# A graph kernel's prologue: four buffers of attribute slices, two of them in A, and the bias of A's tiles added on GpSimd

## The chip, the cores and the metric

The kernel runs on one NeuronCore of a Trainium2 chip. Its metric is the device time of one execution in microseconds (us). Five engines work beside each other, each with its own list of instructions: TensorE (PE, with PEld for its weight loads), VectorE (DVE), ScalarE (ACT), GpSimd (POOL) and SyncE (SP, which here only issues DMAs). They are ordered by semaphores alone.

## The reference

Layer norm and ReLU, then two relational graph layers, then an attention layer over the same edges:

```
edge_type = argmax(edge_attr[:, 16:26])          # one of 10, for 400000 edges
seg  = dst * 10 + edge_type                      # dst is sorted, 12500 nodes
mean = segment_sum(x[src], seg) / max(count(seg), 1)
h    = relu(einsum('nrd,rdo->no', mean, w_rel1) + x @ root1 + b1)
x    = x + (einsum('nrd,rdo->no', mean', w_rel2) + h @ root2 + b2)
x    = x + attention over the same edges          # softmax per destination
```

The kernel first multiplies each node's row by all ten relation weights (a table, ytab) and by the root weight, and then gathers and sums table rows over the edges. An edge's weight is one over the number of edges of its destination and type.

## The kernel before

`prologue()` prepares everything for the first gather pass. Three strands of work run in it at once.

*VectorE, the slices.* The edges lie on 125 partitions, 3200 to each, in 50 slices of 64. A slice holds 64 edges x 42 attributes per partition (1.34 MB in all). SP loads slice t into `ea[t % 2]` by two DMAs (L246) once VectorE has read slice t - 2 (semaphore `s_rel`). VectorE finds the largest of ten attributes (L328), marks it (L329), and turns the mark into a type number (L331 to L333). From slice 5 on, four counts of the edges at a partition's two ends follow (`end_counts`, L321). Between slices stands side work: after slice 1 the destinations (L335 to L349, which wait for dst and for the neighbours' destinations), after slice 3 the step tables (L351 to L380), after slice 6 the sources, and after the slices named in `SHOWN` the statistics of seven tiles of x (L304, L307), with their inverse two slices later.

*VectorE, the rounds.* When all slices are through, the counts are summed (L396), carries between the partitions are made, keys are turned by TensorE and copied by ScalarE (L553, L485), and then ten rounds follow, one for each type: a comparison (L417), a scan forward (L419), a scan backward (L420) and a predicated copy (L422), each over 3200 columns. The rounds 0 to 6 end with the statistics of the next seven tiles, which wait for x. Last come five reciprocals (L430), whose results TensorE turns and ScalarE copies.

*The tile stream.* 98 tiles of 128 nodes, in batches of seven. ScalarE normalizes seven tiles (L458), TensorE turns them (L532) and multiplies each by the ten relation weights and the root weight (L542 to L544), and adds the bias by a product of a row of ones and the bias row (L545). ScalarE copies the ten relation parts to one of two buffers `yb` (L474, L476) and the root part with the bias to A, columns 128 i to 128 i + 127 (L478). GpSimd waits for that and issues the store of `yb` to ytab (L285). ScalarE's copy of tile i waits for the store of tile i - 2 (`s_out`). TensorE's product of tile i waits for ScalarE's last copy of tile i - 2 (`s_y1`). The load of x for batch b + 2 is issued by ScalarE after the fourth tile of batch b. After tile 34 (the end of batch 4) TensorE waits for the end of the slices, for the carries and the keys, before it goes on with tile 35.

Within an engine the order is that of the code. SP's list is one queue of loads: slices, dst, the last destination of each group of 640 edges (625 single elements, L250), the neighbours' destinations (L252, L253), src, and at last the step tables.

`Chain` (called `link`) gives each VectorE instruction a semaphore and waits for it before the next. The gather passes after the prologue start when all engines are through it.

Of the kernel before, what the change touches and what calls it, by code (L numbers as in the profile page):

```python
# [21 lines left out]
ALU = mybir.AluOpType  # L22
# [4 lines left out]
P = 128  # L27
N = 12500
D = 128
# [8 lines left out]
G = 5  # L38
# [6 lines left out]
SHOWN = (7, 15, 23, 31, 39, 46)  # L45
# [38 lines left out]
assert all(BLOCK * (NBLK - 2) + OUT_AT[b] >= GROUPS + OB * b + OB - 1 for b in range(OUTS))  # L84
assert AHEAD == UNROLL and NT % 2 == 0 and STEPS + UNROLL <= SCOLS * P
# [3 lines left out]
def build(nc, x, src, dst, attr, w_rel1, root1, b1, w_rel2, root2, b2, w_l, w_r, att, bias, out,  # L89
# [58 lines left out]
    with outer:  # L148
# [20 lines left out]
        def prologue():  # L169

            with ExitStack() as st:
                ea_all = sbuf(st, "ea", [CH, 2 * EB * ATTR])
                ea = [ea_all[:, k * EB * ATTR:(k + 1) * EB * ATTR] for k in range(2)]
                top = sbuf(st, "top", [CH, EB])
# [30 lines left out]
                brow = sbuf(st, "t1_b", [1, D])  # L205
# [15 lines left out]
                s_ea = [sem(f"ea_in{k}") for k in range(2)]  # L221
                s_dst, s_src, s_nb = sem("dst_in"), sem("src_in"), sem("neighbours_in")
                s_last, s_rel, s_iota = sem("last_in"), sem("ea_used"), sem("iotas")
                s_const, s_raw = sem("prep_const"), sem("raw_free")
# [4 lines left out]
                s_eps, s_w = sem("t1_eps_set"), sem("t1_w_in")  # L229
# [7 lines left out]
                with nc.Block() as block:  # L237

                    @block.sync
                    def _(sp):  # L240
                        av = attr.rearrange("(p t e) a -> p t (e a)", t=CE // EB, e=EB)
                        for t in range(CE // EB):
                            if t >= 2:
                                sp.wait_ge(s_rel, t - 1)
                            for p0, p1 in EA_PARTS:
                                sp.dma_start(ea[t % 2][p0:p1, :], av[p0:p1, t, :]).then_inc(s_ea[t % 2], 16)  # L246
                            if t == 0:
                                sp.dma_start(raw[:, :], dst.rearrange("(p e) -> p e", p=CH)).then_inc(s_dst, 16)
                                with nc.allow_non_contiguous_dma(reason="one destination of each group and chunk"):
                                    sp.dma_start(last_i, dst.rearrange("(a g e) -> a g e", a=1, e=GE)[:, :, GE - 1]).then_inc(s_last, 16)  # L250
                                    sp.wait_ge(s_const, 1)
# [23 lines left out]
                    @block.gpsimd  # L275
                    def _(pool):
                        nc.gpsimd.iota(cols[:, :], [[1, P]], base=0, channel_multiplier=0, allow_small_or_imprecise_dtypes=True).then_inc(s_iota, 1)
                        nc.gpsimd.iota(rowid[:, :], [[0, 1]], base=0, channel_multiplier=1, allow_small_or_imprecise_dtypes=True).then_inc(s_iota, 1)
                        nc.gpsimd.iota(falling[:, :], [[-1, NREL]], base=NREL, channel_multiplier=0, allow_small_or_imprecise_dtypes=True).then_inc(s_iota, 1)
                        nc.gpsimd.iota(gnum, [[1, GROUPS]], base=0, channel_multiplier=0, allow_small_or_imprecise_dtypes=True).then_inc(s_iota, 1)  # L280
                        nc.gpsimd.iota(snum[:, :], [[P, SCOLS]], base=0, channel_multiplier=1, allow_small_or_imprecise_dtypes=True).then_inc(s_iota, 1)
                        nc.gpsimd.memset(rel_all[:, TILES:TILES + SLOTS * G], 0.0).then_inc(s_iota, 1)
                        for i in range(NT):
                            pool.wait_ge(s_y1, i + 1)
                            pool.dma_start(ytab[i * P:(i + 1) * P, :], yb[i % 2]).then_inc(s_out[i % 2], 16)  # L285

                    @block.vector
                    def _(dve):
                        link = Chain(dve, "prep_chain")
                        v = nc.vector  # L290
                        v.memset(eps[:, :], EPS).then_inc(s_eps, 1)
# [32 lines left out]
                        for t in range(CE // EB):  # L324
                            dve.wait_ge(s_ea[t % 2], 16 * len(EA_PARTS) * (t // 2 + 1))
                            a = ea[t % 2][:, :].rearrange("p (e a) -> p e a", a=ATTR)[:, :, EMB:EMB + NREL]
# [7 lines left out]
                            if t == 1:  # L334
                                dve.wait_ge(s_dst, 16)  # L335
                                link(v.tensor_copy(dstc, raw[:, :]))
                                v.engine_nop().then_inc(s_raw, 1)
# [12 lines left out]
                            if t == 3:  # L350
# [30 lines left out]
                            if t == 6:  # L381
# [49 lines left out]

                    @block.scalar
                    def _(act):
# [35 lines left out]
                        def out_rows(i):  # L469
# [7 lines left out]
                            act.wait_ge(s_y0, i + 1)  # L477
                            a.activation(A[:, i * D:(i + 1) * D], py[k][:, NREL * D:ALL], ACT.Copy).then_inc(s_y1, 1)  # L478
# [12 lines left out]
                        act.dma_start(brow[:, :], b1.rearrange("(a d) -> a d", a=1)).then_inc(s_w, 16)  # L491
# [3 lines left out]
                        act.wait_ge(s_eps, 1)  # L495
# [26 lines left out]
                    def _(pe):  # L522
# [12 lines left out]
                        def product(i):  # L535
# [8 lines left out]
                            t.matmul(py[k][:, 1024:ALL], lhs, wt[:, 1024:ALL], start=True, stop=False)  # L544
                            t.matmul(py[k][:, NREL * D:ALL], ones[0:1, :], brow[0:1, :], start=False, stop=True).then_inc(s_m1, 1)  # L545
# [1158 lines left out]
```

## Time and profile before

| | us |
|---|---|
| median of 3 runs | 12709.82 |
| lowest and highest | 12708.29 and 12718.36 |
| the profiled execution | 12666.73 |
| its span | 12664.9 |

The prologue is the first 665 us of the span. Busy over the whole span are TensorE 7165.4 us, VectorE 5372.7, ScalarE 4183.5 and GpSimd 9039.3; nearly all of GpSimd's is the issue of gathers after the prologue. A row of the timeline gives the start in us from the span's start, the duration, the engine, the line, the operation and the tiles it writes and reads; what stands in brackets is the idle time before it and who ended it. A row of waits gives the total in us, how many times, and the longest.

### The profile page before, as it was taken

The page shows a single profiled execution, that of the slowest core. Times are in us where ns is not written, and L with a number is a line of the kernel's source. Part 1 is how long each engine was busy: PE and PEld are TensorE (multiplying, and loading weights), DVE is VectorE, ACT ScalarE, POOL GpSimd, SP SyncE. Part 2 cuts the span into 40 slices and gives each one's busy share as a digit, 9 for nine tenths or more (in the row PEclk, how much of TensorE's full clock was granted, in tenths as well). Part 3 has the DMA queues.
Part 4 walks back from the last instruction along what each step waited for, and adds up shares of the span by engine and source line. Part 5 has one row for each costly group of instructions (what it writes and reads, how often), then busy time and mean ns, then how long its engine had stood idle before and what let it go on. Part 6 is the DMA issues. An engine that isn't in the chain of part 4 may idle for free. (4 is left out here: it accounts for less than half of the span.)

```text
span 12664.9 us, 190403 instructions
## 1 busy us (share of the span) xinstructions
PE 7165.4 (57%) x34895; PEld 5988.6 (47%) x34896; DVE 5372.7 (42%) x11674; ACT 4183.5 (33%) x12473; POOL 9039.3 (71%) x9581
## 2 busy tenths in 40 slices
PE   3734444444444864444444444556777777777777
PEld 1333333333333543333333333445666666666666
DVE  7832222222222641111111111453766766666667
ACT  2522222222222222222222222224444444444442
POOL 0167777777777767777777777767777777777776
PEclk8855555555555975555555555667989999989898
DMA  8611111111112531111111111236888888888887
GB/s 246 207 52 52 53 52 53 52 53 52 53 52 64 187 130 52 53 52 53 52 53 52 53 52 53 75 86 179 236 233 233 237 235 235 235 234 237 233 236 212
DMA packets 922698, 1589.79 MB, mean 126 GB/s; under 512 B 303128, under 2 KB 487318, under 8 KB 915334
## 3 DMA queue, kind: packets, MB, share of 16 engines
q0 software_dynamic: 314112, 685.63, 20.1%
q1 hardware_dynamic: 384568, 595.99, 15.1%
q10 hardware_dynamic: 223412, 301.41, 8.0%
q8 instruction: 219, 3.59, 0.1%
q14 instruction: 387, 3.17, 0.1%
HBM read 1213.18 MB, written 367.39 MB: 125 GB/s over the span
## 5 line engine op out<-in xcount | busy, mean ns | idle before, releaser
L714 POOL DMA_INDIRECT p_g<-ytab,p_i x6250 | 5903.3, 945 | 1971.2 <-issue 1631.1
L1165 POOL DMA_INDIRECT a_g<-xlw,a_i x3125 | 2992.3, 958 | 996.4 <-issue 887.3
L678 PE MATMUL p_pg<-p_v,p_oh 128*128 x6120 | 1343.7, 398 | 1550.4 <-ACT p_v L761 1548.7
L761 ACT ACTIVATE p_v<-p_g,wgt_all 128x128 f32<-128x128 f32 x6250 | 1960.4, 389 | 543.2 <-issue 523.2
L678 PEld LDWEIGHTS p_pg<-p_v,p_oh 128*128 128x128 f32 x6120 | 1203.8, 296 | 1711.3 <-issue 1701.5
L755 ACT ACTIVATE p_i<-rel_all 128x5 int32 (+1 forms) x1250 | 260.1, 208 | 5053.6 <-DMA p_g<-ytab,p_i 5053.6
L678 PE MATMUL p_pt<-p_v,p_oh 128*128 x4200 | 979.8, 417 | 1269.3 <-ACT p_v L761 1269.3
L678 PEld LDWEIGHTS p_pt<-p_v,p_oh 128*128 128x128 f32 x4200 | 877.7, 313 | 1368.3 <-issue 1368.3
L1628 PE MATMUL a_px<-a_g,ident 128*128 x1450 | 736.6, 593 | 849.4 <-SPq L1216 741.2
L616 DVE TENSOR_TENSOR p_oh<-p_cols,local 128x640 f32<-128x640 f32 x1460 | 1195.4, 819 | 24.9
L1264 ACT ACTIVATE a_away<-a_dst,a_minus 128x640 f32 x727 | 602.2, 828 | 1386.7 <-issue 843.5
L635 DVE TENSOR_TENSOR A<-p_pg,A 128x128 f32 x612 | 177.6, 290 | 1988.3 <-PE p_pg L678 1986.6
L1617 PE MATMUL a_pg<-a_v,a_into 128*128 128x132 f32 x7000 | 968.6, 288 | 87.9 <-issue 43.0
L1617 PEld LDWEIGHTS a_pg<-a_v,a_into 128*128 128x128 f32 x7000 | 897.7, 201 | 100.3 <-issue 63.5
L678 PE MATMUL y_py<-p_v,p_oh 128*128 x2080 | 490.0, 420 | 649.5 <-ACT p_v L761 649.5
L635 DVE TENSOR_TENSOR A<-p_pt,A 128x128 f32 x420 | 122.4, 291 | 1669.8 <-PE p_pt L678 1669.5
L678 PEld LDWEIGHTS y_py<-p_v,p_oh 128*128 128x128 f32 x2080 | 438.1, 316 | 699.9 <-issue 699.3
L1634 PEld LDWEIGHTS a_px<-a_xr,a_onto 128*128 128x128 f32 x4350 | 710.4, 220 | 68.4
L1634 PE MATMUL a_px<-a_xr,a_onto 128*128 128x132 f32 x4350 | 707.1, 306 | 0.0
L1628 PEld LDWEIGHTS a_px<-a_g,ident 128*128 128x128 f32 x1450 | 240.0, 207 | 937.6 <-issue 936.7
L1551 DVE TENSOR_TENSOR a_relu<-a_relu,a_pcon 128x640 f32<-128x640 f32 x725 | 587.2, 810 | 175.3 <-ACT a_relu L1314 172.3
L1313 ACT ACTIVATE a_relu<-a_px 128x384 f32<-128x384 f32 x725 | 350.6, 484 | 900.3 <-PE a_py L1634 880.6
(254 smaller groups left out, 9807.6 us busy)
## 6 DMA issues: line engine op xcount, KB each, us to landing
a_xj<-xjw ACTq DMA_DIRECT2D x725, 330.0 KB
xjw<-a_g SPq DMA_DIRECT2D x625, 330.0 KB
a_dst<-in_dst_dram SPq DMA_DIRECT2D x625, 320.0 KB
p_g<-ytab,p_i POOLq DMA_INDIRECT x6250
ytab<-steps POOLq DMA_DIRECT2D x98, 640.0 KB, 3.5
ytab<-src_i SPq DMA_DIRECT2D x98, 640.0 KB
ea<-in_edge_attr_dram SPq DMA_DIRECT2D x50, 1176.0 KB
a_g<-xlw,a_i POOLq DMA_INDIRECT x3125
```

What stands on the lines that cost most here:

```text
L616: v.tensor_tensor(onehot[k][:, :].rearrange("p (t n) -> p t n", t=G), colsp[:, 0:P].rearrange("p (a n) -> p a n", a=1).to_broadcast([P, G, ...
L635: v.tensor_tensor(A[:, ds(to[k], width)], pg[b][:, 0:width], A[:, ds(to[k], width)], ALU.add).then_inc(s_acc, 1)
L678: last = t.matmul(pg[b][:, 0:width], onehot[(at + k) % LOOK][:, q * P:(q + 1) * P], V[:, ds(to + q * width, width)], start=(q == 0), stop= ...
L714: pool.indirect_dma_start(gbuf[k][:, q * D:(q + 1) * D], None, rows, bass.IndirectOffsetOnAxis(ap=stage[k][:, q:q + 1], axis=0)).then_inc( ...
L761: last = a.activation(V[:, c:c + D], gbuf[k][:, q * D:(q + 1) * D], ACT.Copy, scale=wgt[:, ds(G * g + q, 1)])
L1165: pool.indirect_dma_start(gbuf[k][:, q * W:(q + 1) * W], None, xlw, bass.IndirectOffsetOnAxis(ap=stage[k][:, q:q + 1], axis=0)).then_inc(s ...
L1264: a.activation(away[:, :], dall[:, ds(at, GE)], ACT.Abs, bias=minus[:, ds(s, 1)]).then_inc(s_away, 1)
L1313: a.activation(lk[:, 0:HEADT, :], x3[:, :, 0:D], ACT.Relu)
L1551: v.tensor_tensor(lk, lk, attp.rearrange("p (a d) -> p a d", a=1).to_broadcast([P, G, D]), ALU.mult).then_inc(s_wt, 1)
L1617: last = t.matmul(sums(j, b), into[b][:, q * P:(q + 1) * P], V[b][:, q * W:(q + 1) * W], start=(q == 0), stop=(q == G - 1))
L1628: t.matmul(px[b], ident[:, :], gath[:, ds(ring, HEADT * W)], start=True, stop=False)
L1634: last = t.matmul(to, onto[b][:, q * P:(q + 1) * P], xr[k % RING][:, :], start=False, stop=q in (HEADT - 1, G - 1))
```

## The change

Four things change, all in the prologue.

1. Slices go round in four buffers. Two are the old ones, two lie in A's columns of tiles 56 to 97. ScalarE waits for the end of the slices before it writes tile 56.
2. SP issues the first four slices ahead of dst and the single elements; the work on the destinations moves from slice 1 to slice 3, the step tables from slice 3 to 5, the sources from 6 to 8, and the statistics by one or two slices. The semaphores `s_raw` and `s_eps` are merged into others.
3. TensorE's bias product goes. The bias is loaded to all 128 partitions (`biasb`), and GpSimd adds it to A's tile after it has issued that tile's store.
4. GpSimd's block stands behind VectorE's in the text, with its order inside unchanged.

```diff
-SHOWN = (7, 15, 23, 31, 39, 46)
+SHOWN = (9, 16, 24, 32, 40, 47)
+SLICES = 4
+LENT = (NT // BT // 2 + 1) * BT
...
+                ea += [A[0:CH, LENT * D + k * EB * ATTR:LENT * D + (k + 1) * EB * ATTR] for k in range(SLICES - 2)]
...
-                            if t >= 2:
-                                sp.wait_ge(s_rel, t - 1)
+                            if t >= SLICES:
+                                sp.wait_ge(s_rel, t - SLICES + 1)
...
-                            if t == 0:
+                            if t == SLICES - 1:
                                 sp.dma_start(raw[:, :], dst.rearrange("(p e) -> p e", p=CH)).then_inc(s_dst, 16)
...
-                            if t == 2:
-                                sp.wait_ge(s_raw, 1)
+                            if t == SLICES + 4:
+                                sp.wait_ge(s_ev, 1)
                                 sp.dma_start(raw[:, :], src.rearrange("(p e) -> p e", p=CH)).then_inc(s_src, 16)
...
+                        for i in range(NT):
+                            pool.wait_ge(s_y1, i + 1)
+                            pool.dma_start(ytab[i * P:(i + 1) * P, :], yb[i % 2]).then_inc(s_out[i % 2], 16)
+                            if i == 0:
+                                pool.wait_ge(s_w, 48)
+                            here = A[:, i * D:(i + 1) * D]
+                            nc.gpsimd.tensor_tensor(here, here, biasb[:, :], ALU.add)
...
+                            if i == LENT:
+                                act.wait_ge(s_rel, CE // EB)
                             a.activation(A[:, i * D:(i + 1) * D], py[k][:, NREL * D:ALL], ACT.Copy).then_inc(s_y1, 1)
...
-                            t.matmul(py[k][:, 1024:ALL], lhs, wt[:, 1024:ALL], start=True, stop=False)
-                            t.matmul(py[k][:, NREL * D:ALL], ones[0:1, :], brow[0:1, :], start=False, stop=True).then_inc(s_m1, 1)
+                            t.matmul(py[k][:, 1024:ALL], lhs, wt[:, 1024:ALL], start=True, stop=True).then_inc(s_m1, 1)
```

## Rows read from the trace of the kernel before

**Rows 1.** Waits of VectorE, 0 to 392 us: total us, times, longest.

```profile
DVE top L328 <- DMA ea<-in_edge_attr_dram: 74.5, 28, 26.9
```

**Rows 2.** The same view, 0 to 100 us.

```profile
DVE top L328 <- DMA ea<-in_edge_attr_dram: 46.5, 4, 26.9
```

**Rows 3.** Windows: length, busy us (instructions) by engine, clock, DMA share, GB/s.

```profile
0.00:40.00 40.00, 0.00 (x0) 0.01 (x1) 4.55 (x11) 1.30 (x2) 1.40 (x10) 1.00 0.75 181
150.00:375.00 225.00, 132.22 (x273) 58.94 (x274) 187.89 (x531) 66.95 (x141) 16.48 (x31) 0.70 0.99 305
```

**Rows 4.** Timeline of the start, SP's queue and VectorE.

```profile
2.94 20.21 SPq L252 DMA_DIRECT2D edge_i<-in_dst_dram  x1
8.91 0.82 DVE L328 TENSOR_REDUCE top<-ea 125x64 f32<-125x640 f32 x1 [6.56 <-DMA ea<-in_edge_attr_dram]
39.15 0.82 DVE L328 TENSOR_REDUCE top<-ea 125x64 f32<-125x640 f32 x1 [26.95 <-DMA ea<-in_edge_attr_dram]
42.48 1.83 DVE L336 CAST local<-src_i 125x3200 f32<-125x3200 int32 x1
```

**Rows 5.** Timeline of VectorE, one slice.

```profile
128.96 0.82 DVE L328 TENSOR_REDUCE top<-ea 125x64 f32<-125x640 f32 x1
129.81 0.82 DVE L329 TENSOR_TENSOR vote<-ea,top 125x640 bf16<-125x640 f32 x1
134.42 0.82 DVE L328 TENSOR_REDUCE top<-ea 125x64 f32<-125x640 f32 x1
```

**Rows 6.** Timeline of VectorE, from the last slice to the first round.

```profile
375.02 0.82 DVE L328 TENSOR_REDUCE top<-ea 125x64 f32<-125x640 f32 x1 [1.95 <-DMA ea<-in_edge_attr_dram]
391.16 0.36 DVE L396 TENSOR_REDUCE ends<-endc 125x20 f32<-125x200 f32 x1
415.56 1.83 DVE L417 TENSOR_SCALAR local<-relc 125x3200 f32<-125x3200 bf16 x1 [12.00 <-PE t_psum L553]
```

**Rows 7.** Timeline of VectorE, one round and the end of the last.

```profile
437.50 1.80 DVE L417 TENSOR_SCALAR local<-relc 125x3200 f32<-125x3200 bf16 x1
446.45 6.88 DVE L420 TENSOR_TENSOR_SCAN wgt_all<-same,runs 125x3200 f32<-125x3200 bf16 x1
453.37 3.73 DVE L422 COPY_PREDICATED ea<-local,wgt_all 125x3200 f32<-125x3200 int32 x1
641.70 20.20 DVE L430 RECIPROCAL ea<-ea 125x640 f32<-125x640 f32 x5
```

**Rows 8.** Waits of VectorE, 400 to 645 us.

```profile
DVE t_st L304 <- DMA t_x<-in_x_dram: 13.0, 6, 3.3
```

**Rows 9.** Timeline of TensorE, one tile of the stream.

```profile
626.30 1.12 PE L542 MATMUL t_psum<-t_w,t_ht 128*128 128x512 f32 x2
628.86 0.48 PE L545 MATMUL t_psum<-t_b,ones 1*128 1x128 f32 x2
629.28 1.12 PE L542 MATMUL t_psum<-t_w,t_ht 128*128 128x512 f32 x2
```

**Rows 10.** The stores L285, 400 to 640 us.

```profile
DMA to landing us min/median/max: 3.2/3.2/6.6
```

**Rows 11.** Timeline of VectorE and GpSimd near the end of the kernel.

```profile
12534.44 1.30 POOL L1181 TENSOR_TENSOR a_v<-a_xj,a_kept 128x640 f32<-128x640 f32 x1 [0.95 <-PE a_pg L1617]
12534.71 2.11 DVE L1420 TENSOR_TENSOR_SCAN a_fwd<-a_apart,a_s 125x512 f32<-125x512 f32 x1
12535.69 1.14 POOL L1184 COPY a_v<-a_kept 128x20 f32<-128x20 f32 x1
```

**Rows 12.** VectorE's scan L1420: duration ns min/median/max, first and last start.

```profile
L1420 DVE TENSOR_TENSOR_SCAN a_fwd<-a_apart,a_s x29: 1210/1215/2111, 8723.3 to 12534.7; 125x512 f32<-125x512 f32 x29
```

**Rows 13.** GpSimd's copy L1184, the same columns.

```profile
L1184 POOL COPY a_v<-a_kept x49: 198/273/1140, 12520.6 to 12656.7; 128x20 f32<-128x20 f32 x49
```

**Rows 14.** VectorE's addition L1447, one in the timeline and all.

```profile
12551.26 1.37 DVE L1447 TENSOR_TENSOR a_whole<-a_df,a_dl 4x125 f32<-4x125 f32 x1
L1447 DVE TENSOR_TENSOR a_whole<-a_df,a_dl x29: 271/271/1371, 8753.2 to 12551.3; 4x125 f32<-4x125 f32 x29
```

More of the change, by code:

```diff
@@ L84 @@
 assert all(BLOCK * (NBLK - 2) + OUT_AT[b] >= GROUPS + OB * b + OB - 1 for b in range(OUTS))
+assert (SLICES - 2) * EB * ATTR <= (NT - LENT) * D
 assert AHEAD == UNROLL and NT % 2 == 0 and STEPS + UNROLL <= SCOLS * P
@@ L204, in prologue @@
                 wt = sbuf(st, "t1_w", [P, ALL])
-                brow = sbuf(st, "t1_b", [1, D])
+                biasb = sbuf(st, "t1_b", [P, D])
                 xin = [sbuf(st, f"t1_x{k}", [P, BT * D]) for k in range(2)]
@@ L219, in prologue @@
                 early = [range(q, min(q + 4, CT)) for q in range(0, CT, 4)]
-                s_ea = [sem(f"ea_in{k}") for k in range(2)]
+                s_ea = [sem(f"ea_in{k}") for k in range(SLICES)]
                 s_dst, s_src, s_nb = sem("dst_in"), sem("src_in"), sem("neighbours_in")
                 s_last, s_rel, s_iota = sem("last_in"), sem("ea_used"), sem("iotas")
-                s_const, s_raw = sem("prep_const"), sem("raw_free")
+                s_const = sem("prep_const")
                 s_tp, s_ev = sem("turned"), sem("to_turn")
@@ L273, in _ @@
                         sp.wait_ge(s_step, 192)
[L275 to L285, printed above, removed]
                     @block.vector
@@ L290, in _ @@
                         v = nc.vector
-                        v.memset(eps[:, :], EPS).then_inc(s_eps, 1)
+                        v.memset(eps[:, :], EPS).then_inc(s_const, 1)
                         link(v.memset(ones[:, :], 1.0))
@@ L380, in _ @@
                                 v.engine_nop().then_inc(s_tab, 1)
-                            if t == 6:
+                            if t == 8:
                                 dve.wait_ge(s_src, 16)
@@ L430, in _ @@
                             v.reciprocal(c, c).then_inc(s_inv, 1)
+                    @block.gpsimd
+                    def _(pool):
+                        nc.gpsimd.iota(cols[:, :], [[1, P]], base=0, channel_multiplier=0, allow_small_or_imprecise_dtypes=True).then_inc(s_iota, 1)
+                        nc.gpsimd.iota(rowid[:, :], [[0, 1]], base=0, channel_multiplier=1, allow_small_or_imprecise_dtypes=True).then_inc(s_iota, 1)
+                        nc.gpsimd.iota(falling[:, :], [[-1, NREL]], base=NREL, channel_multiplier=0, allow_small_or_imprecise_dtypes=True).then_inc(s_iota, 1)
+                        nc.gpsimd.iota(gnum, [[1, GROUPS]], base=0, channel_multiplier=0, allow_small_or_imprecise_dtypes=True).then_inc(s_iota, 1)
+                        nc.gpsimd.iota(snum[:, :], [[P, SCOLS]], base=0, channel_multiplier=1, allow_small_or_imprecise_dtypes=True).then_inc(s_iota, 1)
+                        nc.gpsimd.memset(rel_all[:, TILES:TILES + SLOTS * G], 0.0).then_inc(s_iota, 1)
+                        counted = 6
+                        for i in range(NT):
[5 more added lines that the diff above has]
+                            nc.gpsimd.tensor_tensor(here, here, biasb[:, :], ALU.add)
                     @block.scalar
@@ L494, in _ @@
                         early_out(src_i, len(early))
-                        act.wait_ge(s_eps, 1)
+                        act.wait_ge(s_const, 1)
                         deviation(0)
```

17 lines of the change are left out of this document (8 added, 9 removed).

## The prediction

> **What bounds the kernel now.** The change touches only the prologue, so the first question is which engine carries it. I read the waits of VectorE first. In the stretch before 392 us it stood idle for attribute slices for 74.5 us at 28 slices [rows 1], and 46.5 us of that fell into the first 100 us at only 4 of them [rows 2]. Between 150 and 375 us the DMA engines were at a share of 0.99 and moved 305 GB/s, while VectorE was busy 188 of 225 us [rows 3]: the two are nearly balanced there, and both matter.
>
> The timeline of the start shows how the early waits come about: the queue of SP was stuck 20.2 us on one issue (from 2.94 us), so the load of slice 1 went out after 23 us; slice 0 was used from 8.91, slice 1 from 39.15, and at 42.48 VectorE began on the destinations [rows 4]. Later a slice with its four end counts takes 134.42 - 128.96 = 5.46 us; its longest instruction with two SBUF inputs, L329, 0.82 [rows 5]. The last slice starts at 375.02, the end counts are summed at 391.16, and the ten relation rounds begin at 415.56 [rows 6]; the 24.4 us between are carries and turned keys, which the change leaves alone.
>
> One round is L417 (1.80 us), two scans (6.9 us each), L422 (3.73) and the statistics of the next seven tiles; the last round ends when the reciprocals start, at 641.70 [rows 7]. So the last stage lasts 641.70 - 415.56 = 226.1 us on VectorE. The waits of that stage show 13.0 us of VectorE idle for the load of x, six times [rows 8]. That load is issued by ScalarE after the fourth tile of a batch, so here the tile stream (TensorE, ScalarE, GpSimd's store) holds VectorE a little. A tile of the stream takes 629.28 - 626.30 = 2.98 us on TensorE, of which the bias product is 629.28 - 628.86 = 0.42 [rows 9]; the store is issued by GpSimd and lands 3.2 us after its issue in the median, up to 6.6 [rows 10]. After the prologue nothing changes. VectorE's end of the prologue moves the end of the kernel one to one.
>
> **The change part by part.**
>
> *Four slice buffers, side loads later.* Four slices, x, the weights and the destinations are 5.4 + 0.5 + 0.7 + 1.6 = 8.2 MB. In the first 40 us the engines moved 181 GB/s at a share of 0.75 [rows 3]; without the idle quarter that is some 200 to 240, so the destinations land at 34 to 41 us, and I take 41. The two edge loads are queued behind the 625 single elements as before and land a few us later. VectorE then starts on them at about 45 us instead of 42.48, with four slices done instead of two. From that point to 391.16 it needed 348.7 us; of these 41.0 were waits for slices (74.5 less the 6.56 and 26.95 before the first two), and two slices are already done (2 x 3.33, from 39.15 to 42.48). That leaves 348.7 - 41.0 - 6.7 = 301.0, and the end at 346 us if no slice is ever late. Against that stand the DMA engines: some 95 MB must move before the last slice lands (50 slices of 1.34, 33 tiles of ytab of 0.66, the rest x, dst, src and weights), and with ten slices, dst, src and weights (18 MB) in by 80 us the other 77 MB at 305 GB/s end near 335, 16 us before VectorE is through. The two limits nearly coincide, so I leave 6 us of waits (bounds 0 and the 28 us that are waited for after 100 us now). The neighbours' wait moves from slice 1 to slice 3 and the keys of src from slice 6 to 8, behind loads that are there by then: nothing. Slices 2 and 3 of the ring lie in A's columns of tiles 56 and later. ScalarE's new wait before tile 56 costs nothing, since TensorE waits for the end of the slices before tile 35 already. The first wait on the constants: nothing.
>
> *The bias product goes.* TensorE's tile falls from 2.98 to 2.56 us. Alone this would take the 13.0 us of waits for x away: the stream needs 7 x 0.42 = 2.9 us less per batch, more than the 2.2 us waited per round. The rest would be slack behind VectorE.
>
> *GpSimd's add.* No add of 128 columns is in the trace. The nearest rows are L1181 with 640 columns at 1.30 us, and the copy of 20 columns at 0.20 [rows 11, 13]: (1.30 - 0.20) / 620 x 108 + 0.20 = 0.39 us. Bounds: 0.2 and 1.3. By time alone 98 x 0.39 = 38 us would lie beside an engine that does little else in the prologue. But the add stands in GpSimd's queue ahead of the next tile's store, and it reads the same memory as VectorE. The end of the kernel shows what that means. At 12534.71 VectorE's scan met L1181 and took 2.11 us instead of 1.215, and GpSimd's copy, asked for at 12535.69, took 1.14 instead of 0.20: each waited for the other to end [rows 11 to 13]. At 12551.26 an addition that takes 0.271 took 1.37, behind L1181 that had come in ahead of it between two VectorE instructions [rows 14]: I read that who waits gets in at the next boundary.
>
> In the front the instructions with two inputs are short (0.82 us at most). 35 adds cost VectorE between 0 and 35 x 0.39 = 13.7 us; the share of such instructions is somewhat over half, I take 8. The front ends at 346 + 6 + 8 = 360 instead of 391: 31 us earlier.
>
> In the last stage both scans (6.9) and L422 (3.7) read two inputs, so an add waits up to 6.9 us, the store of the next tile goes out only after it, and ScalarE needs the store of two tiles earlier to have landed. Worked through for a round, with x the end of a batch's fourth tile: the load of x lands at +4 and the statistics run to +6, L417 and the first scan from +8 to +15, the second scan to +22.5, L422 to +26.5. Two or three tiles get through before +8. Then one store is let out at +15.5, one at +23, one at +27, and each lets ScalarE go on 3.5 us later. The next batch's fourth tile ends at +28.4 if the sixth tile's add comes in before the scan, at +32.1 if it just misses. I take 30 us for such a round, against (226.1 - 3 x 19.7) / 7 = 23.9 now. VectorE meets this as waiting for x. Round 0 has no such wait, the statistics of the second load begin at 52.9 after the stage's start, five rounds of 30 follow, then 2 us and three rounds of 19.7 + 3 x 0.39 = 20.9: 52.9 + 150 + 2 + 62.7 = 268 against 226: 42 us more. Bounds: -13 (adds that hinder nobody), and +53 (all rounds at 32.1). The last stores then land near the end of the rounds, and the reciprocals (20 us, one input) cover the rest.
>
> The Trainium skill, "SBUF — State Buffer", section "Who interferes with whom", speaks against this edit: a VectorE instruction with two SBUF inputs and a GpSimd instruction that reads SBUF exclude each other for the whole instruction. The trace agrees for scans of 1.2 us; that a scan of 6.9 us holds for its full length no run here shows yet. By the page the last stage is the +42; by the weaker reading, in which long scans let an add through, it is the -13.
>
> **Sum.** -31 + 42 = +11 us. The profiled execution (12666.7 us, span 12664.9) would be 12678; its 43 us below the median I take over unchanged: 12709.8 + 11 = 12721.
>
> **The rivals.**
>
> *The adds hinder nobody.* For it: GpSimd is idle nearly all of the prologue, the add is short, and one with a scan of 6.9 us was never seen. Against it: rows 11 to 14. Then the front gives at least 31 and the last stage 13: -44, 12666 us.
>
> *The DMA engines hold the front* (the other side). The place is the stretch from 100 to 375 us, share 0.99. With four buffers a slice is asked for earlier but no byte moves faster, and the stores of ytab compete; the 28 us of later waits stay. Only the early waits give: 46.5 less what remains (6.6, and 45 - 8.9 - 4 x 3.3 = 22.9) is 17, less 8 for the adds is 9. With the last stage at +42 the kernel is 33 us slower: 12743. It decides once the rate while stores and loads mix stays under about 285 GB/s, at which 77 MB take the 16 us longer that eat half of the gain. For it: the share. Against it: the longest of the waits lie before 100 us, where the engines had room (181 GB/s over the first 40 us).
>
> *The spare buffers do nothing* because of the wait before tile 56: excluded by the order of TensorE named above, at most 2 in 100.
>
> **How the numbers follow.** Forecast 0.50, from 12696 to 12747 on its own (-14 to +37: front -20 to -40, last stage +26 to +53). Adds that hinder nobody 0.25, DMA-held front 0.25. A difference under about 0.2% (25 us) can't be told from none here. Faster: all of the first rival and 3 of the forecast's 50, 0.28. Slower: most of the second rival and 5 of the forecast's, 0.25. Same: 0.47. Range: from 12664, which takes in the first rival, to 12752.
>
> **What would show it.** Right if: VectorE's waits for slices fall from 74.5 to 30 to 40 us, nearly all before 45 us; L396 starts near 360 us; L419 and L420 have a maximum of about 7.3 us; GpSimd's adds have a median far over 0.4 us in the last stage and maxima near 7; VectorE's waits for x rise from 13 to some 40 us; the stage from the first L417 to the first reciprocal takes 255 to 280 us. The forecast is wrong if the adds stay at 0.4 us while scans run, if the waits for x vanish, or if L396 still starts after 375 us. The DMA rival is right if waits for slices after 100 us stay above 20 us.

## The result and the profile after

The changed kernel takes 12743.94 us (median of 14 runs, 12722.24 to 12764.93), the kernel before on the same chip 12709.14 (14 runs, 12697.64 to 12718.36): ratio 1.0027, 95% interval 1.0019 to 1.0034. It is 35 us slower. Forecast were 11 us slower (12721, with a range of its own up to 12747), and "same" at 0.47; the number is nearly that of the second rival (12743, chance 0.25).

Three starts on VectorE split the prologue, as in [rows 6, 7]: the sum of the end counts (L387 after, L396 before), the first round (L408, before L417) and the first reciprocal (L421, before L430). From the timeline of VectorE, after:

```profile
388.04 0.36 DVE L387 TENSOR_REDUCE ends<-endc 125x20 f32<-125x200 f32 x1
423.23 1.83 DVE L408 TENSOR_SCALAR local<-relc 125x3200 f32<-125x3200 bf16 x1 [18.73 <-PE t_psum L562]
690.28 4.15 DVE L421 RECIPROCAL ea<-ea 125x640 f32<-125x640 f32 x1
```

The front ends 3.1 us earlier (391.16 to 388.04; forecast 31). The way to the first round grew from 24.4 to 35.2 us (forecast: no change). The last stage grew from 226.1 to 267.1 (forecast 268). At the reciprocals the profiled execution is 48.6 us behind that of before, and its first gather starts as much later (714.2 against 665.6). That is more than the medians say (34.8, interval 24 to 43), and the rest is not explained; the way from the ends sum to the rounds, which differs between 24 and 35 us in the profiles below, is the loosest of the three.

The front, in the waits of VectorE: first 0 to 100 us, then from 100 us to the ends sum (total us, times, longest):

```profile
DVE local L328 <- DMA src_i<-in_dst_dram: 11.2, 1, 11.2
DVE top L320 <- DMA ea<-in_edge_attr_dram: 10.0, 2, 7.1
DVE edge_f L331 <- DMA edge_i<-in_dst_dram: 8.2, 1, 8.2
DVE top L320 <- DMA A<-in_edge_attr_dram: 6.2, 2, 3.4
...
DVE t_st L296 <- DMA t_x<-in_x_dram: 15.2, 3, 12.6
DVE top L320 <- DMA ea<-in_edge_attr_dram: 7.7, 8, 1.4
DVE top L320 <- DMA A<-in_edge_attr_dram: 7.7, 9, 1.4
```

Slices are waited for 31.6 us, against 74.5 [rows 1]. That part did what was forecast (30 to 40). But three waits stand there that before had not: for dst, for the edge columns and for x, 34.6 us together. All waits of VectorE up to the ends sum fell from 78.7 only to 70.6 us; the ends sum less its waits, VectorE's own work, rose from 312.5 to 317.4.

Where the edge wait comes from is in the timeline of the queues of SP and ScalarE, 0 to 45 us:

```profile
4.62 0.89 SPq L254 DMA_DIRECT2D wgt_all<-in_dst_dram  x1
5.56 35.96 SPq L256 DMA_DIRECT2D edge_i<-in_dst_dram  x1
41.57 1.77 SPq L257 DMA_DIRECT2D edge_i<-in_dst_dram  x1
43.38 1.85 SPq L250 DMA_DIRECT2D ea<-in_edge_attr_dram  x1
...
1.85 37.41 ACTq L500 DMA_DIRECT2D t_w<-in_L_gnn_root_dram  x1
```

The issue that held SP 20.21 us before [rows 4] holds it 35.96 now. The second edge load can't go out before 41.57, and slice 4 not before 43.38. The windows that answer to [rows 3], same columns:

```profile
0.00:40.00 40.00, 0.00 (x0) 0.01 (x1) 13.18 (x25) 0.02 (x1) 1.40 (x10) 1.00 0.83 193
150.00:375.00 225.00, 114.25 (x202) 48.97 (x202) 186.22 (x513) 62.11 (x130) 31.27 (x58) 0.70 0.99 285
```

The DMA engines are at 0.99 as before and move 285 GB/s instead of 305. The lower mean comes mostly from the end of the window. From 200 to 300 us both kernels move 303 GB/s; from 360 to 375 us it is, before and after:

```profile
360.00:375.00 15.00, 8.77 (x21) 4.39 (x22) 12.30 (x36) 7.49 (x17) 1.59 (x3) 0.73 0.98 321
...
360.00:375.00 15.00, 5.31 (x7) 1.83 (x6) 12.69 (x43) 2.92 (x6) 1.03 (x2) 0.61 0.69 68
```

SP issues the eight stores of the step tables' columns from 336.28 to 388.86 us there; before it did so from 365.05 to 394.46.

The last stage, from 423 us: waits of VectorE, GpSimd's add (duration ns min/median/max), VectorE's two scans and its predicated copy:

```profile
DVE t_st L296 <- DMA t_x<-in_x_dram: 52.8, 6, 10.1
...
L438 POOL TENSOR_TENSOR A<-A,t_b x98: 464/467/7067, 133.8 to 701.5; 128x128 f32<-128x128 f32 x98
...
L410 DVE TENSOR_TENSOR_SCAN runs<-same,carc,local x10: 6887/6887/7080, 425.3 to 672.4; 125x3201 f32<-125x3201 bf16 x10
...
L411 DVE TENSOR_TENSOR_SCAN wgt_all<-same,runs x10: 6892/6892/6896, 432.2 to 679.5; 125x3200 f32<-125x3200 bf16 x10
...
L413 DVE COPY_PREDICATED ea<-local,wgt_all x10: 3767/3774/3792, 439.1 to 686.5; 125x3200 f32<-125x3200 int32 x10
```

Waits for x rose from 13.0 [rows 8] to 52.8 us, 39.8 of the 41.0 that the stage lost. Adds that meet a scan take up to 7.07 us instead of 0.47. The timeline of GpSimd in one round, with VectorE's two scans, shows what stands behind them:

```profile
509.30 0.56 POOL L434 DMA_DIRECT2D ytab<-steps  x1 [5.74 <-ACT A L488]
509.77 6.89 DVE L410 TENSOR_TENSOR_SCAN runs<-same,carc,local 125x3201 f32<-125x3201 bf16 x1
509.88 7.01 POOL L438 TENSOR_TENSOR A<-A,t_b 128x128 f32<-128x128 f32 x1
516.69 6.89 DVE L411 TENSOR_TENSOR_SCAN wgt_all<-same,runs 125x3200 f32<-125x3200 bf16 x1
516.85 0.56 POOL L434 DMA_DIRECT2D ytab<-steps  x1
517.42 6.40 POOL L438 TENSOR_TENSOR A<-A,t_b 128x128 f32<-128x128 f32 x1
523.78 0.56 POOL L434 DMA_DIRECT2D ytab<-steps  x1
```

An add that begins just behind the start of a scan ends 0.2 us after that scan does. Each store goes out only when the add before it is through, one per long VectorE instruction instead of one per 3 us.

### The profile page after: what moved, and what is told of

Its sections match the earlier page's. It is cut to its first block and busy times, and to the rows that moved or that the text cites. A ratio compares the mean times of both kernels' runs of the same rounds, so it can differ in the third digit from the quotient of the medians.

```text
span 12725.5 us, 190110 instructions
## 1 busy us (share of the span) xinstructions
PE 7149.6 (56%) x34699; PEld 5976.6 (47%) x34700; DVE 5383.6 (42%) x11674; ACT 4176.0 (33%) x12473; POOL 9221.2 (72%) x9679
## 3 DMA queue, kind: packets, MB, share of 16 engines
q1 hardware_dynamic: 384568, 595.99, 15.2%
```

## The experiments

Two theories stood at the start. **L**: an add waits out VectorE's long two-input instructions, the table's store waits behind it, and so the last stage loses its 41 us; in the front the four buffers gain nothing because something else is late. **V**: the adds slow VectorE itself. For the front two more: **Q**, the queue of SP behind the one-element loads; **D**, the DMA engines, where slices, x and table stores share one rate.

All twelve runs are timed against the kernel before on the same chip: 15564 to 15567 us there for the first eight (the passes behind the prologue are some 2880 us longer on those two chips, the prologue is not), 12670 for the next three, 12687 for the last. Ratios are compared, and stages by profile:

| | own work | waits 0-100 | waits 100 to ends | ends sum | to first round | last stage |
|---|---|---|---|---|---|---|
| before | 312.5 | 50.7 | 28.0 slices | 391.2 | 24.4 | 226.1 |
| after | 317.4 | 40.1 | 15.4 slices, 15.2 x | 388.0 | 35.2 | 267.1 |
| e1_buffers | 312.3 | 38.1 | 26.1 slices, 10.3 x | 386.8 | 29.9 | 223.7 |
| e2_add | 318.1 | 51.6 | 26.1 slices | 395.8 | 24.4 | 265.6 |
| e3_write_only | 312.5 | 39.6 | 33.5 slices, 9.5 x | 395.5 | 35.4 | 223.4 |
| e4_act_store | 314.5 | 37.4 | 46.5 x, 20.3 other | 418.6 | 24.6 | 229.3 |
| e8_before_side_pool | 312.5 | 41.8 | 37.6 slices | 391.9 | 24.4 | 224.5 |
| e6_side_pool | 313.0 | 42.4 | 23.6 x | 379.0 | 24.4 | 229.1 |
| e7_late_tables | 313.1 | 42.7 | 18.3 x | 374.1 | 24.4 | 232.8 |
| e5_short_stores | 313.0 | 44.4 | 9.0 x | 366.4 | 24.4 | 238.7 |
| e9_few_rows | 313.0 | 42.5 | 9.0 x | 364.5 | 24.4 | 262.4 |
| e10_five_batches | 310.3 | 42.2 | 13.6 slices | 366.2 | 24.4 | 229.2 |
| e11_add_front | 318.6 | 38.3 | 8.1 slices, 29.3 x | 394.4 | 30.1 | 224.8 |
| e12_before_five | 310.4 | 52.2 | 24.6 slices | 387.1 | 24.4 | 227.7 |

The waits are the sums of VectorE's view of waits up to the ends sum; own work is the ends sum less them. It is one profile each: after, e1_buffers and e11_add_front have nearly the same front, and their late waits are 30.6, 36.4 and 37.4 us. Up to the ends sum, after and e11_add_front are even the same program, and yet they differ by 6.4 us there and by 5.1 us in the way to the first round. A difference of that size in one front shows little by itself.

**The two halves of the change.** e1_buffers is the changed kernel with the bias by TensorE, e2_add the kernel before with GpSimd's add alone:

```diff
 # e1_buffers, against the changed kernel
-biasb = sbuf(st, "t1_b", [P, D])
+brow = sbuf(st, "t1_b", [1, D])
...
-nc.gpsimd.tensor_tensor(here, here, biasb[:, :], ALU.add)
...
-t.matmul(py[k][:, 1024:ALL], lhs, wt[:, 1024:ALL], start=True, stop=True).then_inc(s_m1, 1)
+t.matmul(py[k][:, 1024:ALL], lhs, wt[:, 1024:ALL], start=True, stop=False)
+t.matmul(py[k][:, NREL * D:ALL], ones[0:1, :], brow[0:1, :], start=False, stop=True).then_inc(s_m1, 1)
 # e2_add, against the kernel before: the same lines the other way round
```

> The change without its third part: four slice buffers and the later side work stay, the bias is again added by TensorE's product and GpSimd only issues stores. Theory (the port shared by GpSimd's add and VectorE's scans holds the stores): the last stage, from the first relation comparison to the first reciprocal, falls from 267 us back to 226 to 230; the front keeps what the changed kernel shows (end counts summed near 388 us, rounds begin near 423), so 12700 to 12722 us. Rival (four buffers in A themselves slow the stage, or the loss sits in the front): the last stage stays above 250 us and the time near 12740.

Measured: ratio 0.9999 (0.9991 to 1.0008). The rounds began at 416.7, not near 423.

> The kernel before with the third part alone: two slice buffers and the old side work, the bias added by GpSimd to A's tiles. Theory: the last stage is some 267 us instead of 226 and the front as before within 5 us, so 12709 + 41 to 48 = 12750 to 12757 us. Rival (the loss needs both parts, because the four buffers push the tile stream back): under 12730 us and a last stage under 245.

Measured: ratio 1.0038 (1.0025 to 1.0051), from half as many runs as the others: 60 us in the medians, 44 at the reciprocals of the profile. The last stage is 39.5 us longer with the add alone and no longer with the buffers alone, so the loss of that stage is the add's. The buffers alone gain 4.4 us at the ends sum and give them back by the first round. In e2_add's last stage, waits of VectorE and the add:

```profile
DVE t_st L308 <- DMA t_x<-in_x_dram: 51.1, 6, 8.6
...
L289 POOL TENSOR_TENSOR A<-A,t_b x98: 465/579/7076, 133.4 to 697.0; 128x128 f32<-128x128 f32 x98
```

**Is it the lock, and is it the store behind it?** e3_write_only puts an instruction that only writes in the add's place (it leaves out bias and root product); e4_act_store keeps the adds and moves the stores out from behind them.

```diff
 # e3_write_only, against the changed kernel
-here = A[:, i * D:(i + 1) * D]
-nc.gpsimd.tensor_tensor(here, here, biasb[:, :], ALU.add)
+nc.gpsimd.memset(A[:, i * D:(i + 1) * D], 0.0)
 # e4_act_store, against the changed kernel
-pool.dma_start(ytab[i * P:(i + 1) * P, :], yb[i % 2]).then_inc(s_out[i % 2], 16)
...
 act.wait_ge(s_y0, i + 1)
+act.dma_start(ytab[i * P:(i + 1) * P, :], yb[k]).then_inc(s_out[k], 16)
```

> The changed kernel with a memset of A's tile to zero in the place of GpSimd's add: GpSimd still has one instruction per tile between two stores, but it only writes (the bias and the root product are left out of A). Theory (two instructions that read through the shared port exclude each other): the memsets stay at about 0.2 us also while scans run, the last stage falls to 213 to 225 us, the kernel to 12690 to 12712. Rival (any GpSimd instruction that touches SBUF waits for VectorE's scan): maxima near 7 us, last stage near 267, 12740 us.

Measured: ratio 1.0000 (0.9991 to 1.0009), last stage 223.4. Its front is 8.7 us longer than that of e1_buffers (33.5 us of late waits for slices), which no run explains. Its memsets never wait:

```profile
L437 POOL MEMSET A<- x98: 223/223/239, 135.0 to 644.0; 128x128 f32 x98
```

> The changed kernel with the stores of ytab issued by ScalarE, between its copies of the ten relation parts and of the root part; GpSimd only adds. Theory (the loss comes through the store that stands behind a waiting add, not through VectorE): the adds still show maxima near 7 us, VectorE's waits for x in the last stage fall from over 50 us to under 10, the last stage to 213 to 222 us, the kernel to 12690 to 12712. Rival (the adds slow VectorE itself, 0.4 us each): last stage above 235 us whoever issues the stores.

Measured: ratio 1.0023 (1.0011 to 1.0035). The adds wait as long as ever, and the last stage is back at 229.3 with 12.2 us of waits for x:

```profile
DVE t_st L296 <- DMA t_x<-in_x_dram: 12.2, 5, 5.2
...
L437 POOL TENSOR_TENSOR A<-A,t_b x98: 447/458/6972, 136.7 to 672.7; 128x128 f32<-128x128 f32 x98
```

The expected 213 to 222 and "under 10" were missed. Less its waits for x, the stage is 217.1 us of VectorE's own time here, against 213.1 in e1_buffers and before and 214.3 in the changed kernel. So it is the store behind the waiting add that costs nearly all of the 41 us; theory V is left with 1 us of them, and with 4 here. The ratio stays at 1.0023, for another reason too: with ScalarE's stores the front is 30 us longer (46.5 us of waits for x, stores landing after up to 45.6 us).

**Adds in the front alone.** e11_add_front is the changed kernel with the add for tiles 0 to 34 and TensorE's bias from tile 35 on.

```diff
+if i < BT * (len(SHOWN) - 1):
     nc.gpsimd.tensor_tensor(here, here, biasb[:, :], ALU.add)
```

> The changed kernel with GpSimd's adds for tiles 0 to 34 only; from tile 35 on TensorE adds the bias again. Theory L (the adds cost only where VectorE's scans of 6.9 us run): last stage 223 to 230 us as with the bias by TensorE (e1_buffers 223.7), all adds under 2 us, ends sum at 386 to 392 and rounds at 415 to 421, ratio 1.000. Rival (adds in the front delay the table stream too, by holding up stores beside VectorE's 820 ns reduces): ends sum or rounds 5 us or more behind e1_buffers (386.8, 416.7), as in the changed kernel's 423.2.

Measured: ratio 0.9999 (0.9990 to 1.0008), last stage 224.8. The adds' maximum is 949 ns:

```profile
L439 POOL TENSOR_TENSOR A<-A,t_b x35: 464/466/949, 131.9 to 408.6; 128x128 f32<-128x128 f32 x35
```

The cost of the last stage goes with the adds beside the scans, as theory L has it. Theory L's numbers for the front did not come: the ends sum is at 394.4 and the rounds at 424.5, 7.6 and 7.8 us behind e1_buffers. 6.3 of that is VectorE's own work (318.6 against 312.3), which is also 317.4 in the changed kernel and 318.1 in e2_add. 35 adds in the front cost VectorE 5 to 6 us (2 in e4_act_store). The rival's "5 us or more behind" did come, but most of it as VectorE's own time and not through held-up stores.

**The front: queue or DMA engines?** e6_side_pool takes dst, edges and group ends off SP's queue in e1_buffers; e8_before_side_pool does the same with two buffers.

```diff
 # in @block.sync
-sp.dma_start(raw[:, :], dst...); sp.dma_start(last_i, ...); sp.dma_start(edge_i..., ...)  (x2)
 # in @block.gpsimd, behind the iotas
+pool.dma_start(raw[:, :], dst.rearrange("(p e) -> p e", p=CH)).then_inc(s_dst, 16)
+pool.wait_ge(s_const, 2)
+pool.dma_start(edge_i[1:CH, 0:1], ...).then_inc(s_nb, 16)
+pool.dma_start(edge_i[0:CH - 1, 1:2], ...).then_inc(s_nb, 16)
+pool.dma_start(last_i, ...).then_inc(s_last, 16)
```

> e1_buffers (four buffers, bias by TensorE) with the loads of dst, of the two edge columns and of the group ends issued by GpSimd at its start, so that SyncE issues nothing but slices (and src) until the last slice. e1_buffers has its ends sum at 386.8 us and its rounds at 416.7, with 24.8 + 16.8 us of waits for slices, 11.0 for dst, 7.1 for the edges. Theory Q (SyncE's queue: it stands for 36 us behind the one-element loads, and dst and the edges come late for that): the 18 us of waits for dst and edges go, the slices' waits fall by 10 or more, ends sum at 360 to 368, rounds at 390 to 398, ratio 0.9985 to the kernel before. Theory D (the transfers of slices, x and table stores share the 16 DMA engines, and the order of issue moves no bytes): the waits for dst and edges come back as waits for slices, ends sum at 380 to 390, ratio 1.000.

Measured: ratio 0.9991 (0.9983 to 1.0000), ends sum 379.0, rounds 403.4.

> The kernel before with nothing changed but the issuer of dst, edge columns and group ends (GpSimd at its start). The kernel before waits 46.5 us for slices in its first 100 us, 20 us of it while SyncE stands behind these loads. Theory Q: 15 to 25 us of these waits go, with two buffers as well, ends sum at 366 to 378, ratio 0.9985 to 0.999. Theory D: the slices land late anyway, ends sum at 385 to 392, ratio 1.000. If e6_side_pool is no further forward than this kernel, then the two buffers more are worth nothing even where SyncE is free.

Measured: ratio 0.9996 (0.9987 to 1.0006), ends sum 391.9. With two buffers it came as theory D has it (385 to 392, the waits back as waits for slices). With four neither theory had it whole: 379.0 lies between Q's 360 to 368 and D's 380 to 390. The waits for dst and edges went, but the first 100 us are no shorter for it. Waits of VectorE in e6_side_pool, 0 to 100 us, then 100 to 379:

```profile
DVE top L313 <- DMA ea<-in_edge_attr_dram: 18.5, 2, 11.7
DVE rel_all L342 <- PE t_psum L565: 14.7, 1, 14.7
DVE top L313 <- DMA A<-in_edge_attr_dram: 7.3, 2, 4.6
...
DVE t_st L289 <- DMA t_x<-in_x_dram: 23.6, 3, 13.6
```

The 14.7 us have a queue behind them too, ScalarE's. In its list the copies of the turned destinations stand behind its own loads, and one of these issues held it for 50.98 us:

```profile
1.86 50.98 ACTq L495 DMA_DIRECT2D t_w<-in_L_gnn_root_dram  x1
...
59.17 1.28 ACT L490 ACT_TABLE_LOAD   x1 [59.03 <-issue]
60.47 1.07 ACT L490 ACTIVATE dst_all<-t_psum 128x500 f32<-128x500 f32 x1
```

What e6_side_pool won is late: no slice is waited for after 100 us, only x. It is 7.8 us at the ends sum and 13.2 at the rounds against e1_buffers, of which the last stage takes 5.4 back (229.1 against 223.7), and the interval of its ratio reaches none. With two buffers (e8) the 8.9 us saved early came back as waits for slices later (37.6 against 28.0).

**Take traffic out of the front.** In e6_side_pool, e5_short_stores stores 64 of 1280 columns of tiles 0 to 48, e9_few_rows 8 of 128 rows; the rest of these rows gets the weights' numbers during the last stage, so that their last stage and ratio say nothing about the front. e7_late_tables holds the stores of src and of the step tables until the keys are made.

```diff
 # e9_few_rows
+if i < NT // 2:
+    pool.dma_start(ytab[i * P:i * P + 8, :], yb[i % 2][0:8, :]).then_inc(s_out[i % 2], 16)
+else:
     pool.dma_start(ytab[i * P:(i + 1) * P, :], yb[i % 2]).then_inc(s_out[i % 2], 16)
+    pool.dma_start(ytab[(i - NT // 2) * P + 8:(i - NT // 2 + 1) * P, :], wt[8:P, 0:NREL * D]).then_inc(s_nb, 16)
 # e7_late_tables
 sp.wait_ge(s_pa, 2 * len(early))
+sp.wait_ge(s_key, 1)
 sp.dma_start(src_dram, src_i[:, :]).then_inc(s_step, 16)
```

> e6_side_pool with the table stores of tiles 0 to 48 cut to 64 of 1280 columns (their other columns get the weights' numbers later, beside the stores of tiles 49 to 97; the output isn't the reference's). Theory D (bytes bound the front): with 32 MB less to store in the front the waits for slices and x fall under 10 us in sum, ends sum at 345 to 352 and rounds at 372 to 380, 15 to 40 us before e6_side_pool's. Theory Q: the stores hinder no slice, ends sum within 5 us of e6_side_pool's. The last stage gets the stores back, its waits for x may rise.

Measured: ratio 0.9984 (0.9974 to 0.9994), ends sum 366.4.

> e6_side_pool with the table stores of tiles 0 to 48 cut to 8 of their 128 rows, whole rows of 5120 bytes, so that packets keep their size (the other rows get the weights' numbers later; the output isn't the reference's). e5_short_stores took 32 MB out of the front, but in packets of 256 bytes, and its DMA share stayed at 0.95 to 1.00 while the rate fell to 226 to 239 GB/s; its ends sum came at 366.4 against 379.0. Theory D (DMA time bounds the front; 98.47 MB in 391 us in the kernel before): with some 23 MB and their packets gone the DMA share of 100 to 300 us falls under 0.9, waits for x under 6 us, ends sum at 348 to 358. Rival (the front is held by the order of stats, turns and products behind the x loads, not by bytes): ends sum at 364 to 372, as in e5_short_stores.

Measured: ratio 1.0007 (0.9998 to 1.0016), ends sum 364.5, at the near end of the rival's range. 12.6 and 14.5 us came off the ends sum of e6_side_pool, and it is the waits for x that shrank, from 23.6 to 9.0. The 345 to 352 expected of e5_short_stores by theory D could not be reached: 313 us are VectorE's own work and 44.4 the waits of the first 100 us, which no store touches since the first goes out after 130 us. In e9_few_rows the same floor is 355.5, inside theory D's 348 to 358; with 9.0 us of late waits it was missed by 6.5. Windows of e9_few_rows:

```profile
100.00:200.00 100.00, 48.47 (x127) 23.52 (x127) 94.41 (x264) 31.45 (x57) 4.53 (x9) 0.85 0.89 236
200.00:300.00 100.00, 59.32 (x132) 26.68 (x132) 91.73 (x254) 31.88 (x68) 8.01 (x16) 0.74 1.00 231
```

From 200 to 300 us the share stays at 1.00 with fewer bytes, at 231 GB/s. So a share of 1.00 does not by itself say that a transfer is late: no slice was. Over 100 to 300 us the share is 0.95 at 233 GB/s, where theory D wanted it under 0.9; e6_side_pool has 0.97 at 293. The edit took bytes out and hardly any DMA time, so it says little on what freed DMA time would be worth.

> e6_side_pool with SyncE's stores of src and of the step tables (small elements, 341 to 389 us in the changed kernel) held until the keys are made, after the ends sum. Theory T (these stores clog the table stores of tiles 30 to 34, ScalarE waits for them, and the turns that VectorE needs ahead of its rounds come late): the way from the ends sum to the rounds' start falls from 30 us (e1_buffers) towards the 24.4 us of the kernel before, rounds 5 to 10 us before e6_side_pool's. Rival: they clog nothing, the way stays as in e6_side_pool; or they come back in the last stage as waits for x, which then rise from 10 to 20 us.

Measured: ratio 0.9997 (0.9988 to 1.0006), ends sum 374.1, stage 232.8. The way to the first round is 24.4, but it was 24.4 in e6_side_pool already, so theory T gets no support. It wasn't tried in a kernel with the longer way either, and stays open. 4.9 us came off the ends sum and 3.7 returned in the last stage.

**Fewer tiles in the front.** e10_five_batches moves one batch of seven tiles from the front of e6_side_pool to the last stage; e12_before_five does it in the kernel before.

```diff
 # e10_five_batches
-SHOWN = (9, 16, 24, 32, 40, 47)
+SHOWN = (9, 19, 29, 38, 47)
 # e12_before_five
-SHOWN = (7, 15, 23, 31, 39, 46)
+SHOWN = (7, 17, 27, 37, 46)
```

> e6_side_pool with five in place of six of the fourteen batches of rows in the front (stats after slices 9, 19, 29, 38, 47), nine in the last stage. Theory D: 7 stores fewer (4.6 MB, about 15 us at 300 GB/s) and one stats block of 7 us fewer for VectorE: ends sum at 360 to 368, and the last stage, with one stats block more, 236 to 242 instead of 229, if the last tiles' copies (7 tiles behind the ninth round) don't hold the weights' turn; sum 0 to 8 us better than e6_side_pool, ratio to the kernel before 0.9985 to 0.999. Rival: the table's last tiles become the end, the first gather comes 10 us or more after the reciprocals' usual 24 us, and the prologue is as long as e6_side_pool's or longer.

Measured: 12646.54 us against 12670.02, ratio 0.9979 (0.9970 to 0.9988): 23 us faster than the kernel before, and the best of all. The reciprocals start at 619.78, 21.9 us before 641.70 [rows 7]:

```profile
619.78 4.15 DVE L414 RECIPROCAL ea<-ea 125x640 f32<-125x640 f32 x1
```

The ends sum came 12.8 us earlier and the stage stayed at 229.2, shorter than the expected 236 to 242: VectorE waits for x 13.7 us in it, with nine stats blocks in ten rounds, and a block is less work than the 7 us it was taken for (the front's own work fell by 2.7 us).

> The kernel before with one line changed: five of the fourteen batches of rows in the front (stats after slices 7, 17, 27, 37, 46), two buffers of slices and the side loads where they were. In e10_five_batches (four buffers, side loads from GpSimd) the ends sum came 12.8 us before e6_side_pool's, and its last stage took 229 us. Theory D (the DMA engines hold the front: fewer stores in it, less waiting): here too the waits for slices fall from 74.5 by 8 to 13 us, VectorE's own work from 312.5 to 310, ends sum at 376 to 381, last stage 226 to 229, ratio 0.9988 to 0.9995. Rival (with two buffers each slice comes late by its own round trip, whatever else moves; it is the buffers that let e10_five_batches use what the stores left): waits for slices 70 or more, ends sum at 386 or later, ratio 0.9998 to 1.0005.

Measured: ratio 1.0000 (0.9991 to 1.0009), ends sum 387.1, waits for slices 72.5. Those are the rival's numbers: with two buffers the waits for slices hardly shrink (74.5 to 72.5) when there are fewer stores. Its waits after 100 us:

```profile
DVE top L328 <- DMA ea<-in_edge_attr_dram: 24.6, 21, 2.8
```

Four buffers alone (e1), the side loads alone (e8) and the fewer tiles alone (e12) are each worth nothing that can be measured; the three together are worth 23 us. The first two without the third (e6) are worth some 11 us, with an interval that reaches none.

## Why the prediction was right and wrong

**Right: the last stage.** +42 was forecast, +41.0 measured, by the mechanism described: adds of up to 7 us (7.07), adds with a median of 1.27 us in the stage, waits for x at 40 us (52.8, a rise of 39.8), rounds of 30 us (the six after the first took 30.3 to 32.1, by the starts of L408). e2 shows that the add does it alone, e4 that it is the store queued behind it, e3 that an instruction that only writes doesn't wait. The first rival is refuted. The Trainium skill, "SBUF — State Buffer", section "Who interferes with whom", held for scans of 6.9 us too (adds of up to 7.07 us), which [rows 11] could not show.

**Right in size, wrong in one place: what the adds cost VectorE.** Each add was taken at 0.39 us on the other side too. In the front 8 us were forecast and 5 to 6 measured (e2, e11, after). In the last rounds 0.39 per add was added to three rounds; but the scans' medians did not move (6.887, 6.892), the predicated copy grew from 3.73 to 3.77. Of VectorE's own time the 41 us hold about 1 (214.3 against 213.1).

**Wrong: the front, -31 forecast, -3.1 measured at the ends sum.** The step that failed is "that leaves 301.0, and the end at 346 us if no slice is ever late", with "I leave 6 us of waits". The slices' waits fell by 42.9 us, as in the forecast. By its own sign, an ends sum after 375 us, the forecast is wrong here. The sum looked at the slices alone, and the time went into four places:
- The edges: "the two edge loads are queued behind the 625 single elements as before and land a few us later". They were called "behind loads that are there by then: nothing" and cost 8.2 us of waiting: the issue behind the single elements took 35.96 us instead of 20.21, with four slices issued ahead of it instead of one. That this is why it took longer is not shown. VectorE began on the destinations at 42.91 (forecast 45) and stood again right behind.
- The slices behind the four: SP was free for slice 4 only at 43.38. Early waits fell from 50.7 to 40.1, by 10.6 us, where the second rival had 17.
- Later waits: 28.0 before, 30.6 after, forecast 6. Half are for slices and half for x, which was not in the forecast at all. From e6's 23.6, removing store traffic (e5, e9) or a batch (e10) takes 10 to 15 us, so the table's stores are a part of the cause.
- The adds, 4.9 us (forecast 8).

Together -10.6 + 2.6 + 4.9 = -3.1.

Two sums of the prediction don't come out either. From 335 to 346 are 11 us, not the "16 us before VectorE is through"; and the bounds -20 and +53 make +33 (12743), not +37 (12747).

**Wrong: "24.4 us ... which the change leaves alone".** They became 35.2. The front's last tiles were still in the stream: the last one was copied at 409.65 us, 22 us after the ends sum, and before at 387.21, ahead of it. VectorE waited 4.31 us for TensorE to turn the counts, a wait that the kernel before doesn't have, and 18.73 instead of 12.00 us for the turned keys, whose copies stand behind those tiles on ScalarE. ScalarE in turn waited for its stores, 27.0 us from 375 to 410:

```profile
389.43 1.02 ACT L482 ACTIVATE steps<-t_psum 128x1024 f32<-128x1024 f32 x1 [13.99 <-DMA ytab<-steps]
400.78 1.02 ACT L482 ACTIVATE steps<-t_psum 128x1024 f32<-128x1024 f32 x1 [7.05 <-DMA ytab<-steps]
408.32 1.02 ACT L482 ACTIVATE steps<-t_psum 128x1024 f32<-128x1024 f32 x1 [5.93 <-DMA ytab<-steps]
```

This comes with the four buffers (e1 29.9, e3 35.4, e11 30.1) and not where the side loads are elsewhere (e6, e7, e10: 24.4). A part of it is in the change itself: the last statistics of the front moved from slice 46 to 47 and begin 26.4 us ahead of the ends sum instead of 33.4. That alone isn't enough, since e6 has 26.0 and its way is 24.4. Why the stores land so late just then is not settled. Theory T of e7 (the step tables' stores clog those of the table) fits in part: the step tables' stores begin at 336 us here (338 in e1, 345 in e3, 334 in e11) and only at 364 in e4, which has 24.6 with its side loads on SP. But they begin at 328 in e6.

**The second rival** gave nearly the number, 12743, but not by its mechanism, and that is luck. Its sum was -9 + 42; measured were -3.1, +10.8 on the way to the first round, which it had at nothing, and +41.0, which make 48.7 in the profile against 34.8 in the medians. Its sign was "waits for slices after 100 us stay above 20 us": they were 15.4, the other half of the late waits being for x. Its condition, a rate "under about 285 GB/s", is not clearly met: the window's mean of 285 stands at its edge, but from 100 to 200 us the rate is 263 (274 before) and from 200 to 360 us 303 to 308 (302 to 303 before). The forecast's own range to 12747 holds the time by the same luck: its front, -20 to -40, did not come.

What held the front is shown in part only. From 100 us on less store traffic takes up to 14.6 us of waits away (e6 to e9). In the first 100 us e6 freed SP's queue, and the waits were 42.4 us against 38.1 in e1; ScalarE's queue, which stood for 50.98 us then, was left as it was.

Not tried: the step tables' stores held back in e1_buffers, where the way is long; ScalarE's loads of the weights moved, so that the 14.7 us wait of e6 and e10 goes; the adds put behind the last scan; any of these combined with e10.

## What to carry to other kernels

Before crediting a wait's removal, subtract all waits of the engine from the stage's end: what is left (312.5 us here) is the floor as long as the work is the same, and each other transfer that must land in the stretch is a candidate for the next wait, not only the one whose buffers were doubled. An instruction that can be locked out by another engine must not stand ahead of anything urgent in its queue; put it behind, or on a queue of its own. A buffer more is worth what the issuing queue and the traffic beside it let through, so such edits are tried together before one is given up.

## What the hardware showed that was not expected

- A GpSimd add waiting behind VectorE's two-input scans took 7.07 us instead of 0.47, but cost those scans nothing in the median (6.887 us; the longest 7.080). Beside these scans the pause is one-sided in the main. It is not so everywhere: in [rows 14] it is VectorE's addition that waited for GpSimd, 1.37 us instead of 0.271, and 35 adds beside the short instructions of the front cost VectorE 5 to 6 us. A memset of the same tile takes 223 ns with or without scans (maximum 239).
- A single DMA issue can hold its engine's queue for long: 20.21 and 35.96 us on SP, behind 625 single elements (before, after), and 19.16, 37.41 and 50.98 us on ScalarE (before, after, e6; the last behind no more loads of its own than the first). What sets these times is not shown.
- The DMA share says little of the rate: 1.00 at 231 GB/s in e9_few_rows and 0.98 at 303 before, both from 200 to 300 us, and 0.69 at 68 from 360 to 375 us after.
- Table stores issued by ScalarE instead of GpSimd (e4) landed after up to 45.6 us instead of 25.0, and waits for x in the front rose from 15.2 to 46.5 us.
